# First GAT layer of a four-layer graph network in column groups, and a whole sort moved into the second layer

## The reference, cut to what matters

```python
def gat_layer(x, src, dst, W, a_s, a_d, b, concat):
    h = (x @ W).reshape(N, H, C)                        # H = 2 heads, C = 64
    alpha_s, alpha_d = (einsum('nhc,hc->nh', h, a) for a in (a_s, a_d))
    logits = leaky_relu(alpha_s[src] + alpha_d[dst], 0.2)
    e = exp(logits - segment_max(logits, dst)[dst])
    a = e / segment_sum(e, dst)[dst]
    out = segment_sum(h[src] * a[:, :, None], dst)
    return (out if concat else out.mean(axis=1)) + b
src, dst = concat(src, arange(N)), concat(dst, arange(N))   # a loop of each node to itself
h = gat_layer(x, src, dst, W1, as1, ad1, b1, concat=True)
out = gat_layer(h, src, dst, W2, as2, ad2, b2, concat=False)
x = layernorm(x + out)
```

## Time and profile before

| | |
|---|---|
| the three runs | 4652.38, 4662.45, 4663.33 us; median 4662.45 |
| the profiled execution | 4651.74 us, span 4649.9 us |
| mean granted TensorE clock | 0.533 of full speed |
| busy share of the span | PE 31%, DVE 53%, ACT 21%, POOL 60% |
| first GAT layer | 1412.6 to about 2058 us |
| second GAT layer | 2058 to about 2715 us |

### The profile page before, as it was taken

One profiled execution on the slowest core, in us unless ns is written; L12 is line 12 of the kernel. 1 busy time (PEld: TensorE's weight loads), 2 busy tenths in 40 slices (PEclk: granted clock), 3 DMA queues, 4 the chain that ended last, 5 costly groups with the idle time before them and its releaser, 6 DMA issues. The chain is left out here.

```text
span 4649.9 us, 35089 instructions
## 1 busy us (share of the span) xinstructions
PE 1426.0 (31%) x5413; PEld 1238.2 (27%) x5413; DVE 2475.6 (53%) x5048; ACT 960.7 (21%) x2420; POOL 2782.0 (60%) x2525
## 2 busy tenths in 40 slices
PE   2888177771040002653400000000000057245121
PEld 2888066661030001542300000000000045134121
DVE  4556066660687848762078853334864423353454
ACT  1555044440020000210100011221000024123110
POOL 7777777777206750027750047777248877777687
PEclk9555555555555555655555555555555556556555
DMA  3666155541011100324403345554001145344011
GB/s 82 184 190 194 43 135 138 138 132 37 7 47 37 28 14 23 90 68 104 128 4 91 97 118 146 146 149 135 6 10 19 18 115 157 103 113 131 16 17 17
DMA packets 258339, 398.82 MB, mean 86 GB/s; under 512 B 91231, under 2 KB 95209, under 8 KB 258241
## 3 DMA queue, kind: packets, MB, share of 16 engines
q1 hardware_dynamic: 171022, 322.96, 23.0%
q0 software_dynamic: 87264, 75.37, 9.8%
HBM read 186.08 MB, written 213.11 MB: 86 GB/s over the span
## 5 line engine op out<-in xcount | busy, mean ns | idle before, releaser
L806 PE MATMUL banks<-ident,cross_in 125*2 125x125 f32 (+3 forms) x26 | 10.5, 405 | 1993.8 <-DVE cross_in L829 1341.9
L593 PE MATMUL banks<-node_w,x_t 65*125 65x200 f32 x1600 | 551.9, 537 | 0.0
L806 PEld LDWEIGHTS banks<-ident,cross_in 125*2 125x2 f32 (+3 forms) x26 | 3.0, 116 | 1998.4 <-DVE cross_in L829 1345.0
L593 PEld LDWEIGHTS banks<-node_w,x_t 65*125 65x125 f32 x1600 | 515.8, 330 | 3.4
L215 POOL DMA_INDIRECT edge_rows<-x_rows,src_i x400 | 402.1, 1005 | 129.1 <-issue 129.1
L273 POOL DMA_INDIRECT x_rows<-r_x,src_scat_i x200 | 257.3, 1287 | 122.0 <-issue 122.0
L273 POOL DMA_INDIRECT norm_rows<-edge_rows,scat_i x200 | 257.7, 1288 | 74.2 <-issue 74.2
L273 POOL DMA_INDIRECT out_dram<-n_out,scat_i x200 | 250.9, 1254 | 78.5 <-issue 60.6
L636 DVE TENSOR_REDUCE n_var<-n_sq 125x8 f32<-125x512 f32 x125 | 85.6, 686 | 317.7 <-ACT n_sq L650 317.6
L215 POOL DMA_INDIRECT edge_rows<-x_rows,norm_s x200 | 207.7, 1039 | 64.1 <-issue 64.1
L215 POOL DMA_INDIRECT edge_rows<-in_x_dram,src_i x200 | 205.1, 1025 | 67.7 <-issue 63.7
(11 more groups left out here) (346 smaller groups left out, 5036.7 us busy)
## 6 DMA issues: line engine op xcount, KB each, us to landing
h_rows<-r_h SPq DMA_DIRECT2D x125, 462.0 KB
x_rows<-r_x SPq DMA_DIRECT2D x125, 241.5 KB
x_rows<-r_x SPq DMA_DIRECT2D x125, 224.0 KB
r_x<-x_rows SPq DMA_DIRECT2D x125, 224.0 KB
x_rows<-n_out SPq DMA_DIRECT2D x125, 224.0 KB
n_in<-in_x_dram SPq DMA_DIRECT2D x100, 224.0 KB
n_c<-x_rows SPq DMA_DIRECT2D x100, 224.0 KB
out_dram<-n_out SPq DMA_DIRECT2D x100, 224.0 KB
```

The source lines that it names most:

```text
L593: done = pe.matmul(product[h][:, n // 2, n % 2, :], x_t[u][:, at:at + P], node_w[:, :], start=True, stop=True)
L806: pe.transpose(bank[0][0:cols, 0:rows], frm, ident[0:rows, 0:rows]).then_inc(s_tout, 1)
```

## The change

It does the following.

1. First GAT layer: the columns are worked in four groups of chunks, 0 to 10, 10 to 18, 18 to 22 and 22 to 25 (`GROUPS` loses its border at 24). The softmax is a running one: within a group VectorE keeps the running maximum (`peaks`) and scales the sums so far by the exponential of its step (`running_softmax`), so that a group can be weighed and summed (one scan for each feature and head, now over the group's columns, with the last column of the group before as its initial value) when that group's columns are there. `merge_own` then mixes in the node's own row, and the group's chunks go through TensorE and ScalarE. GpSimd no longer weighs rows in this layer.
2. In a chunk, ScalarE now makes the two products of the own rows (16 instructions of 125x64 with a scale per partition, `own_chunk`), one chunk ahead; VectorE makes two products and two sums. A chunk's mixed rows are also stored to a new table, ED (two DMAs, 500 KB).
3. What crosses partitions is mended at the end of the block (`ends_in`): only the first segment end of each partition can be touched by it; its row is fetched from ED, mended, sent through TensorE again and scattered to H2.
4. The whole sort runs in the second layer's block (`CUT = 0`); in the first layer only the loading of the pairs stays.
5. Every second scan of `sum_rows_dve` is linked, in all layers (`SCANS_BETWEEN = 2`). Keys are compared as integers, without three casts. The norm block gains `first_ends` (10 small VectorE instructions).

```diff
-GROUPS = (0, 10, 18, 22, 24, 25)
+GROUPS = (0, 10, 18, 22, 25)
+SCANS_BETWEEN = 2
-        CUT = STEPS.index(("direct", SLOT_BITS - 1))
+        CUT = 0
...
             for f in range(D):
                 done = dve.tensor_tensor_scan(rows[:, :, f], cont[:, :], rows[:, :, f], 0.0, ALU.mult, ALU.add)
-            v.link(done)
+                if f % SCANS_BETWEEN == SCANS_BETWEEN - 1:
+                    v.link(done)
...
+        def running_softmax(dve, s, rows, at, n, sums, weigh):
...
+            done.then_inc(s.args, 1)
+            dve.wait_ge(s.exps, 2 * n + 1)
...
+            for i in range(*groups[n]):
+                v.link(weigh(dve, slice(i * NC, i * NC + NC)))
+            for h in range(H):
+                for f in range(D):
+                    done = dve.tensor_tensor_scan(sums[h][:, c, f], scales[:, h, c], sums[h][:, c, f], sums[h][:, a - 1, f:f + 1] if a else 0.0, ALU.mult, ALU.add)
+                    if f % SCANS_BETWEEN == SCANS_BETWEEN - 1:
+                        v.link(done)
...
             @block.vector
             def _(dve):
                 sort_fill_dve(dve)
+                own_logits(dve)
                 sort_start_dve(dve)
                 sort_dve(dve, PARTS[0], held[0], held[1])
-                attention_dve(dve, s1, xa, D + 1)
...
+                dve.wait_ge(s_first, 16)
+                for n, (start, end) in enumerate(groups):
+                    dve.wait_ge(s_got[n], got_done(n, 1))
+                    running_softmax(dve, s1, xa, D + 1, n, sums, weigh)
+                    merge_own(dve, s1, n, 1.0)
+                    for i in range(start, end):
...
+                        for h in range(H):
+                            done = dve.tensor_tensor(parts[h][:, :, :], sums[h][:, c, :], wide(mixes[:, h, w]), ALU.mult)
+                        v.link(done)
+                        dve.wait_ge(s1.own, i + 1)
+                        for h in range(H):
+                            done = dve.tensor_tensor(e_dup[u][:, :, h, :], e_dup[u][:, :, h, :], parts[h][:, :, :], ALU.add)
+                        done.then_inc(s1.x, 1)
+                ends_in(dve, s1, sums)
...
+                def own_chunk(i, start):
+                    u = i % 2
+                    act.wait_ge(s1.loaded[u], ROWS_DONE * (i // 2 + 1))
+                    if i >= 2:
+                        act.wait_ge(s1.turned, i - 1)
+                        act.wait_ge(s1.mixed[u], ROWS_DONE * (i // 2))
+                    for c in range(NC):
+                        w = (i - start) * NC + c
+                        for h in range(H):
+                            done = nc.scalar.activation(e_dup[u][:, c, h, :], r_x1[u][:, c, 0:D], ACT.Copy, scale=mixes[:, 2 + h, w:w + 1])
+                    done.then_inc(s1.own, 1)
...
+                for n, (start, end) in enumerate(groups):
+                    logits_act(act, s1, n)
+                    if n:
+                        turned_chunk(start - 1)
+                        row_chunk(start - 2)
+                        row_chunk(start - 1)
+                    merged_act(act, s1, n)
+                    act.wait_ge(s1.args, 3 * n + 3)
+                    own_chunk(start, start)
+                    for i in range(start, end - 1):
+                        own_chunk(i + 1, start)
+                        turned_chunk(i)
+                        if i > start:
+                            row_chunk(i - 1)
...
+                for i in range(ECH):
+                    u = i % 2
+                    sp.wait_ge(s1.x, i + 1)
+                    rows_dma(sp, edge_rows(ED, i // 2, u, 2 * D), flat(e_dup[u][:, :, :, :].rearrange("p c h f -> p c (h f)")), s1.mixed[u])
+                    if i + U < ECH:
+                        load(i + U)
+                    sp.wait_ge(s1.row, i + 1)
+                    rows_dma(sp, edge_rows(H2[0:EDGES], i // 2, u, W2ROW), flat(r_h2[u][:, :, :]), s1.stored[u])
```

More of the change, by code:

```diff
@@ L953, in sort_dve @@
         def sort_dve(dve, part, to_k, to_d):
-            now, turns = 0, turns_before(part[0])
+            now = 0
             for n in range(*part):
@@ L1221, in project_act, with got_done @@
             pairs(nc.scalar, ECH, body)
+        groups = list(zip(GROUPS, GROUPS[1:]))
+        s_got = [sem(f"s_got{n}") for n in range(len(groups))]
+        def got_done(n, passes):
+            return 16 * NC * (groups[n][1] - groups[n][0]) * passes
         s0 = phase("gate", "tanh_in tanh centred squares var dev x1 turned turned_sb terms row", "stored")
@@ L1377, in weigh3 @@
             return eng.tensor_tensor(xc[:, at, :], xc[:, at, :], wide(heads[0][:, at]), ALU.mult)
+        GCOLS = NC * max(end - start for start, end in groups)
+        scales = both_x_t[0:P, 0:4 * J].rearrange("p (k j) -> p k j", k=4)
+        mixes = both_x_t[0:P, 4 * J:4 * J + 4 * GCOLS].rearrange("p (k j) -> p k j", k=4)
+        peaks = both_x_t[0:P, 4 * J + 4 * GCOLS:6 * J + 4 * GCOLS + 2].rearrange("p (h j) -> p h j", h=H)
+        masses = both_x_t[0:P, 6 * J + 4 * GCOLS + 2:8 * J + 4 * GCOLS + 2].rearrange("p (h j) -> p h j", h=H)
@@ new lines, in logits_act, with merged_act, first_at @@
+        def logits_act(act, s, n):
+            a, b = (NC * c for c in groups[n])
+            act.wait_ge(s.args, 3 * n + 1)
+            nc.scalar.activation(scales[:, :, a:b], scales[:, :, a:b], ACT.Exp).then_inc(s.exps, 1)
+        def merged_act(act, s, n):
+            w = NC * (groups[n][1] - groups[n][0])
+            act.wait_ge(s.args, 3 * n + 2)
+            nc.scalar.activation(mixes[:, :, 0:w], mixes[:, :, 0:w], ACT.Exp).then_inc(s.exps, 1)
+        def first_at(dve, plane_of, to):
+            for h in range(H):
+                v.link(dve.tensor_tensor(heads[h][:, :], plane_of(h), first_end[:, :], ALU.mult))
+                done = dve.tensor_reduce(to[:, h:h + 1], heads[h][:, :], AX, ALU.add)
+            v.link(done)
@@ new lines, in _ @@
+                done.then_inc(s1.x, 1)
+                v.link(dve.tensor_scalar(heads[0][:, :], first_end[:, :], 1.0, -1.0, ALU.subtract, ALU.mult))
+                dve.wait_ge(s1.row, ECH + 1)
+                for k in range(4):
+                    v.link(dve.tensor_tensor(own4[:, :, k], own4[:, :, k], heads[0][:, :], ALU.mult))
+                for k in range(4):
+                    v.link(dve.scalar_tensor_tensor(own4[:, :, k], first_end[:, :], first_row[:, 2 * D + k:2 * D + k + 1], own4[:, :, k], ALU.mult, ALU.add))
@@ L1414, in _ @@
             @block.tensor
             def _(pe):
+                over_segments_pe(pe, "hold", 2)
                 sort_pe(pe, PARTS[0])
[L1417 to L1429, removed]
[L1430 to L1439 removed]
@@ new lines, in _ @@
+                for start, end in groups:
+                    for i in range(start, end):
+                        turn_chunk(i)
+                        if i > start:
+                            heads_chunk(i - 1)
+                    heads_chunk(end - 1)
+                ends_pe(pe)
+                pe.wait_ge(s1.x, ECH + 1)
+                pe.wait_ge(s1.turned_sb, ECH)
+                pe.transpose(bank[0][:, 0:P], first_mixed.rearrange("p h f -> p (h f)"), ident[0:P, 0:P]).then_inc(s1.turned, 1)
```

328 lines of the change are left out of this document (223 added, 105 removed).

## The result

Three runs of the changed kernel took 4769.90, 4774.75 and 4784.25 us, median 4774.75, against 4662.45 before: the ratio is **1.0251, 95% interval 1.0218 to 1.0284**. The forecast was 4770 us, slower. The profiled execution is the 4784.25 one (span 4782.4); its span is 132.5 us over that of before.

| us | before | after | measured | forecast |
|---|---|---|---|---|
| up to the first GAT layer | 1412.7 | 1417.4 | +4.7 | +6 |
| first GAT layer | 646.3 | 611.8 | -34.5 | -56 |
| second GAT layer, to the start of its attention | 276.8 | 426.0 | +149.2 | +157 |
| from there to the end | 2314.1 | 2327.2 | +13.1 | +7 |

A forecast was written before the change was run, and what follows sets the result against it. A serial tail behind the first layer's gather was taken as the bound, with the second layer's gather barely hiding the projection. 4651.7 - 56 + 157 + 11 + 2 = 4766, forecast 4770 us, range 4690 to 4830.

The forecast's parts named there:

- The second layer, +157: Second GAT layer: the whole sort delays the projection, so attention starts 434 us into the block instead of 277.5, +157 us.
- the long wait: Projection: one ScalarE wait of 22.19 us, others near 6, falls into the sort, so 16 us are taken off.
- The rival that the projection does not wait: Second layer: projection free of the sort, 157 us would vanish, giving 4610 us; chance 0.02.
- The first layer, -56: First GAT layer worked by groups: the chain ends at 2002 against 2058, -56 us.
- Start: First layer: group 0 can start at 1536, after column 80 is issued, placed and landed.
- VectorE's four groups: First layer: weighing 36, scans 113, pointers 22 and small operations 31 us, sum 203 us.
- Chunk loop: First layer, groups 0 to 2: cycle 12.4 us with transfers bare for 6.0, together 213 us.
- End: First layer, from group 3's mixes to the scatter's landing: 50 us.
- The weighing of own: First-layer chunk loop: ScalarE's 16 own-row instructions with a pointer scale take 3.8 us, ends 1.9 and 3.8.
- The rival with the gain: First-layer loop runs at TensorE's pace: 4679 us at a 7.8 us cycle, 4625 at about 5; chance 0.10, 0.06 faster.
- the longer cycle of 15 us: First-layer chunk loop: ED's 12.8 MB meet gather and H2, 15 us a cycle makes 4815 us; chance 0.13.
- The links: Gate, second GAT and cosine passes: 32 links in each at 0.08 to 0.14 us, +11 us (8 to 13).

The follow-up runs named there:

- Experiment 1: Changed kernel with the sort cut back where it was (merges 1 to 13 in the first layer, the rest in the second): 4704.9 us, 1.0113.
- 3: Changed kernel with the sort cut at merge 11, the steps before it run in the first layer: 4662.3 us, 1.0025.
- 5: Changed kernel with the projection's load of chunk c+2 issued once chunk c is turned, before the wait for its rows: 4716.7 us, 1.0143.
- experiment 7: Changed kernel with ScalarE's own-row scale a constant 0.5 instead of a pointer: 4741.1 us, 1.0196.
- experiment 2: Changed kernel with SyncE in the first layer storing a chunk's H2 rows behind the next chunk's ED store and load: 4692.6 us, 1.0088.
- experiment 8: Kernel before the change with every second scan of sum_rows_dve linked, nothing else changed: 4663.6 us, 1.0036.
- experiment 6: Changed kernel with SyncE's new store order in the first layer, the sort cut at merge 11 and earlier projection loads together: 4549.1 us, 0.9782.
- experiment 4: Changed kernel with SCANS_BETWEEN 64, a link only behind the last scan of a feature loop: 4724.0 us, 1.0170.
- experiment on the pointer of the scans: Changed kernel with each scan started from constant 0.0, without the carry between column groups, on the slower chip: 6546.8 us, 1.0199.
- edits 2 to 5: Changed kernel with SyncE's store order, cut at step 11, links every 64 scans and earlier projection loads: 6363.0 us (0.9905) on the slower chip, 4507.2 us (0.9675) elsewhere.

## Why the prediction was right, and where its steps were off

*The total.* 4770 against 4774.75 is closer than the terms were, and that is in part luck. Between the profiled executions the sum had 114 us and 132.5 were measured: the first layer was off by 21.5, the second by -8, the stretch behind them by 6 and the one ahead by -1. The medians differ by only 112.3, as the profiled execution of before lay 10.7 us under its median and this one 9.5 over.

*The second layer, +157, measured +149.* Sort's end at 262 us of the block (forecast 264), crossing at 424. The projection took 162 us where 168 stood; the long wait was indeed gone: without the first, ScalarE's 24 waits for turned edge attributes were 95.8 us together before (the 22.19 of the earlier trace rows among them) and 75.0 now. Experiment 1 brings back 149 us by the cut alone, 3 brings back 115 by moving part of the sort, 5 brings back 53 by shortening what stood bare. The rival that the projection does not wait is ruled out.

*The first layer, -56, measured -34.5.* The mechanism held, the sizes were off by 21.5 us together:

- Start: group 0 at 1544.9, or 1540.2 once the 4.7 us are taken off by which the block starts later, against 1536. The tail's rows took 10.1 us to land where the earlier trace rows had 3.7: +4.
- VectorE's four groups: 60.3, 59.8, 44.2 and 40.3, together 204.6 against 203: +2. The scans alone were 140 against 135. Pointer 60 ns (forecast 58), link 0.14 us (0.08 to 0.14).
- Chunk loop: 111.3, 81.9 and 30.8, together 224.0 against 213: **+11, the largest miss**. Behind the first, the cycles were 13.2 on the mean instead of 12.4: the transfers lay bare for 7.1 us (6.4 to 8.1), not 6.0; own took 3.9 as forecast (3.8); the copies of turned and row took 2.2, not 2.6 (1648.30 to 1650.47).
- End: 54.7 against 50. ScalarE's last row ended 33.3 us behind the mixes, where 34 stood, and VectorE's crossing, with its wait of 13.67 us behind the last chunk on TensorE's queue, was back before that (2005.71). The miss lies in the last step, 8.9 us from the product's copy (2019.3) to the next block's start (2028.2) where 4 stood: VectorE's last sums ran to 2024.0, and the next block began 4.18 us behind them, which the sum did not hold: +5.

*The weighing of own.* It was taken at 3.8 us from the two instructions of the earlier trace rows; 3.92 was measured, and experiment 7 shows 92 ns for the pointer. The Trainium skill, ScalarE: Activation LUTs, "What ACT_TABLE_LOAD costs", puts it at 93 ns for each pointer operand; the runs agree. The lower end (1.9 us, a copy without one) was too low too: 2.45.

*The rival with the gain.* Its sentence "each us of the cycle is worth about 19 us" was wrong. The sum itself held 7 + 5 + 1 = 13 cycles, and experiment 2 bears that out: 6.4 us less in each make its 84 us. With 13, a cycle of 7.8 gives 4706, not 4679, and the sum meets 4651.7 only at a cycle of 3.6, below what ScalarE's own work takes (3.9 and 2.2). So the loop alone could not make the changed kernel faster than the one before. Experiment 2, at 7.3, was still 1.0088. The rival's price was too good, and its chance of "faster", 0.06, had no cycle behind it. The same factor makes the longer cycle of 15 us 4800 and not 4815. The range's upper end of 4830 was not even the sum of its terms, which is 4820, and 4808 with 13.

*The rest.* The links were +11 in three passes; the gate shows 3.9, and experiment 8 shows 17 us for all passes of the kernel before. Behind the attention 13.1 us were measured against 7. In the changed kernel and the six edits that touch nothing there (experiments 1, 2, 3, 5, 6 and 7), this stretch takes from 2314 to 2328 us, so the last 6 are within that scatter, and I leave them unexplained.

## What to carry to other kernels

Work that is moved under a cover takes its place in front of whatever waits for its end. Before a sort goes "behind a gather", add up everything queued between its end and the first use of the gather: here 162 us of projection. A cut at another step took back 115 of the 149 us lost, and loads issued before the wait for stores took back 53. In a loop that works on several chunks at once, the order on the queue that issues the DMAs is part of the schedule: a store that waits for the end of chunk k must not stand ahead of the load for k+2. Small costs on many short instructions (a pointer, a link) can weigh as much as what a finer split of the work wins: 23 us for pointers on VectorE, 33 on ScalarE and 39 for links, against 34.5 won.

## What the hardware showed that I had not expected

- A link, a wait of VectorE for its own last instruction, costs 0.14 us behind a pair of scans of 64 to 80 columns (experiment 4) and 0.13 behind one of 200 (35.48 less 31.59, by 31).
- A pointer as a scan's initial value costs 60 ns, the same at 24, 32 and 64 columns (experiment on the pointer of the scans). One as ScalarE's scale costs 92 ns at 64 columns, the only length run (experiment 7).
- On one of the four chips of the experiments the three kernels also timed elsewhere took 38 to 41% longer, in stretches: engines stood between instructions while the profile shows nothing that they waited for, or only "remote", and a linked pair of scans came every 2.80 us. The ratios to the kernel before were still 1.0233 against 1.0251 for the changed one. For the one with edits 2 to 5 they were 0.9905 against 0.9675, so a gain measured there does not carry over. What held the instructions back is not shown.
- The granted clock of an execution was near 0.53 or near 0.7, and the time didn't follow it. The two kinds differ in the first 1200 us: 1.00 in experiment 2, 0.54 in experiment 6, and yet the first GAT layer starts at 1413.9 and 1416.3. So the mean clock of an execution says nothing of a stretch; the stretch has to be asked. On the last chip but one the kernel before took 6418 to 6429 us at 0.52 and 6425 and 6434 at 0.72.
